# A two-layer expert network with a recurrence between them on one core: the prologue reordered, four staging buffers for weights, integers in the routed rows

## The reference, cut to what matters

```
x = x + 0.5 * ffn(layernorm(x))
x = x + lru(layernorm(x))
x = x + 0.5 * ffn(layernorm(x))

# ffn: top 2 of 8 experts per token
logits = x @ router_w.T + router_b
topk_val, topk_idx = top_k(logits, 2)
weights = softmax(topk_val)
h1, h2 = split(x @ w1[e].T + b1[e])          # 128 -> 2 * 512
out_e  = (silu(h1) * h2) @ w2[e].T + b2[e]   # 512 -> 128
...
# lru: state_t = Lambda * state_(t-1) + B x_t;  y = Re(C state) + D x
```

## Time and profile before

| what | value |
|---|---|
| median of 3 runs | 672.25 us (671.88 to 679.42) |
| profiled execution | 666.18 us, its span 664.4 us |
| prologue, to TensorE's first expert matmul | 99.86 us |
| first expert stage, to the last output scatter | 99.9 to 297 us |
| recurrence and second routing | 297 to 445.2 us |
| second expert stage | 445.2 to 641 us |
| tail | 641 to 664.4 us |
| busy: TensorE, VectorE, ScalarE, GpSimd | 70%, 64%, 53%, 50% of the span |

### The profile page before, as it was taken

The page is one execution under the profiler, slowest core; times in us unless marked ns, Lnnn a source line. Parts: engine busy times, 40 slices in busy tenths (PEclk is TensorE's granted clock), DMA queues, the critical chain, the costliest instruction groups (busy, mean ns, idle before and its releaser), DMA issues.

```text
span 664.4 us, 16357 instructions
## 1 busy us (share of the span) xinstructions
PE 462.8 (70%) x4580; PEld 408.6 (61%) x4580; DVE 423.0 (64%) x1336; ACT 350.9 (53%) x798; POOL 333.4 (50%) x463
## 2 busy tenths in 40 slices
PE   2433007888899999971988783327879799999910
PEld 2433005676699988860878673216769599989910
DVE  6563564656689996737799384145546477776715
ACT  4656233555577777752253431325457477877720
POOL 1277683545656655560002657604557556565640
PEclk9999999879899999985889786558889799999975
DMA  6142362333323222206000101102333223232228
GB/s 195 53 144 72 113 155 63 73 78 80 65 56 67 60 56 52 60 15 227 27 0 18 49 24 56 50 16 61 80 75 84 61 63 69 53 56 61 54 67 313
DMA packets 94552, 50.17 MB, mean 76 GB/s; under 512 B 81902, under 2 KB 84720, under 8 KB 94484
## 3 DMA queue, kind: packets, MB, share of 16 engines
q1 hardware_dynamic: 85396, 32.31, 20.3%
q0 software_dynamic: 9088, 16.94, 8.0%
HBM read 17.25 MB, written 23.24 MB: 61 GB/s over the span
## 4 chain that ended last, share of the span: by engine, by line
PE 55%; DVE 18%; issue 13%; DMA 5%; ACT 3%; another core or an unknown queue 3%; SPq 1%; POOL 1%; POOLq 0%; DVEq 0%; ACTq 0%
PE bank L1188 11%; PE bank L1189 11%; PE bank L1190 11%; PE bank L1210 5%; PE bank L1208 5%; PE bank L1209 5%; DMA yin<-y 3%; DVE bn L658 2%; DVE xres L909 2%; ACT xn L462 2%; PE bank L1070 1%; PE bank L1202 1%; PE bank L1168 1%; DVE w1l L786 1%
## 5 line engine op out<-in xcount | busy, mean ns | idle before, releaser
L424 POOL DMA_INDIRECT y<-yout,dest x156 | 155.3, 995 | 142.3 <-ACT yout L549 105.7
L993 DVE SCALAR_TENSOR_TENSOR act<-bank,bias,gate 128x256 f32<-128x256 f32 x312 | 146.3, 479 | 105.0 <-ACT gate L531 86.6
L403 POOL DMA_INDIRECT rows<-rows,slot_i x128 | 136.2, 1064 | 149.9 <-DVE slot_i L745 110.2
L1188 PE MATMUL bank<-xt_t,w1h 128*128 128x256 f16 x624 | 176.1, 282 | 26.9 <-DVE w2l L786 13.0
L531 ACT ACTIVATE gate<-bank,bias 128x256 f32<-128x256 f32 x312 | 142.3, 479 | 89.1 <-remote 56.0
L1190 PE MATMUL bank<-xt_t,w1l 128*128 128x256 f16 x624 | 175.7, 282 | 4.9 <-issue 4.9
L1189 PE MATMUL bank<-xt_t,w1h 128*128 128x256 f16 x624 | 175.8, 282 | 4.6 <-issue 4.3
L1210 PE MATMUL bank<-w2h,actl 128*128 x624 | 123.5, 223 | 5.8 <-issue 5.8
L1208 PE MATMUL bank<-w2h,wst 128*128 x624 | 124.9, 223 | 3.5 <-issue 3.0
L1209 PE MATMUL bank<-w2l,wst 128*128 x624 | 123.5, 223 | 2.7 <-issue 2.7
L999 DVE TENSOR_TENSOR actl<-act,wst 128x512 f16<-128x512 f32 x156 | 107.8, 691 | 15.2 <-ACT wst L539 10.3
(11 more groups left out here) (200 smaller groups left out, 552.9 us busy)
## 6 DMA issues: line engine op xcount, KB each, us to landing
yin<-y SPq DMA_DIRECT2D x16, 512.0 KB, 4.8
wst<-in_w_t SPq DMA_DIRECT2D x8, 512.0 KB
y<-yout,dest POOLq DMA_INDIRECT x156
rows<-padrow SPq DMA_DIRECT2D x18, 130.0 KB
xres<-in_x SPq DMA_DIRECT2D x8, 256.0 KB, 3.4
wst<-in_w_t SPq DMA_DIRECT2D x8, 256.0 KB
rows<-rows,slot_i POOLq DMA_INDIRECT x128
out<-xres SPq DMA_DIRECT2D x4, 512.0 KB, 6.8
```

The source lines that it names most:

```text
L403: pool.indirect_dma_start(out=rows_dram[f], out_offset=bass.IndirectOffsetOnAxis(ap=slot_i[:, k, f, g, t:t + 1], axis=0), in_=rows[:, k, g ...
L424: pool.indirect_dma_start(out=y_dram[f], out_offset=bass.IndirectOffsetOnAxis(ap=dest[:, t % STEP, r:r + 1], axis=0), in_=yout[:, t % STEP ...
L993: V.scalar_tensor_tensor(act[:, j, :], up_ps[j][:, SLOT:], bias[:, t % STEP, HB + j:HB + j + 1], gate[:, j, :], ALU.add, ALU.mult).then_in ...
L1188: T.matmul(o, w1h[:, bass.ds(at, P)], xt_t[:, t % STEP, 0, :], start=True, stop=False)
```

## The change

- **Staging**: four buffers (`STAGED = 4`) in place of two. `wst` becomes an arena that also holds `acth`, `actl`, `gate` and `act` of the tiles, which had buffers of their own. SP sends the router's two small loads behind x of group 0, then the rest of x, experts 0 to 3, the other ten small loads, and experts 4 to 7, each waiting for `weight_low(e - 4)`.
- **ScalarE's prologue**: `high_part` goes ahead of `transposed`; `weight_high` of experts 0 and 1 goes between them for groups 2 and 3; 2, 3 and 4 behind the second bias; 5, 6 and 7 at the end.
- **VectorE's prologue**: all groups are measured ahead (`measured`, with `mv` for four groups), `scales` runs one group further ahead than it did, and `weight_low` 0, 1, 2 stand behind slots 1, choice 2 and the tile table, 3 to 7 at the end.
- **GpSimd**: 42 rows ahead of tile 0 in stage one, then two behind each of the tiles 0 to 10; as before in stage two (54, then one per tile). The output index is stored as an integer in the row, so `take_meta` is gone: `send_y` and `weighted` read `meta` itself, which has 8 buffers.
- **Tiles** are written out whole on every engine.
- **Recurrence**: `add_outputs(0, 3)` and its statistics move from behind `recurrence(1)` to behind `recurrence(0)`.

```diff
-        wst = sb("wst", [P, 2, 2 * HID + HB * P])
+        wst = sb("wst", [P, STAGED, 2 * HID + HB * P])
+        arena = wst[:, :, :].rearrange("p i w -> p (i w)")
...
-        mv = sb("mv", [P, 2, GT, 2])
+        mv = sb("mv", [P, 4, GT, 2])
...
+                    for dst, src in route:
+                        sp.dma_start(dst, src).then_inc(s_route, 16)
+            for e in range(NE):
+                if e == STAGED:
                     for dst, src in small:
                         sp.dma_start(dst, src).then_inc(s_small, 16)
-            for e in range(NE):
-                if e >= 2:
-
-                    sp.wait_ge(s_wl, 2 * (e - 1))
...
+                if e >= STAGED:
+
+                    sp.wait_ge(s_wl, 2 * (e - STAGED + 1))
...
-                    wait(sp, s_dest, n(1 - STEP))
-                    sp.dma_start(meta[:, t % STEP, :, :],
+                    wait(sp, s_ysent[t % STEP], dma(STEP - METAS, 32))
+                    sp.dma_start(meta[:, t % METAS, :, :],
...
-            def take_meta(t, n, dma):
-
-                pool.wait_ge(s_meta[t % STEP], dma(STEP, 16))
-
-                wait(pool, s_ysent[t % STEP], dma(0, 32))
-
-                pool.sem_inc(s_xgo, 1)
-                pool.tensor_copy(dest[:, t % STEP, :], meta[:, t % STEP, :, 0])
-                pool.tensor_copy(weight[:, t % STEP, :], meta[:, t % STEP, :, 1]).then_inc(s_dest, 1)
...
-                        out_offset=bass.IndirectOffsetOnAxis(ap=dest[:, t % STEP, r:r + 1], axis=0),
+                        out_offset=bass.IndirectOffsetOnAxis(ap=meta_i[:, t % METAS, r, 0:1], axis=0),
...
+                each = [(g, i) for g in range(BATCH) for i in range(TOPK * GT)]
+                ahead = 2 * TOPK * GT + AHEAD_2 if f == 0 else 3 * TOPK * GT + AHEAD
+                for g, i in each[:ahead]:
+                    send_row(f, g, i)
+                later = iter(each[ahead:])
+
+                def tile(t, n, dma):
+
+                    send_y(f, t, n)
+                    for g, i in islice(later, 2 if f == 0 else 1):
                         send_row(f, g, i)
...
             rows_of(0, 0)
             for g in range(BATCH):
                 if g + 1 < BATCH:
-                    rows_of(0, g + 1)
+                    normalise(number["ffn", 0, g + 1])
+                    high_part(0, g + 1)
+                    if g > 0:
+                        weight_high(g - 1)
+                    transposed(number["ffn", 0, g + 1])
+                else:
+                    second_bias()
+                    for e in range(BATCH - 2, NE - 3):
+                        weight_high(e)
                 exp_dif(0, g)
                 second_row(0, g)
...
-                act_e.wait_ge(s_dest, n(1))
+                act_e.wait_ge(s_meta[t % STEP], dma(STEP, 16))
...
+            together(measured(0))
+            together(scales(0, 1))
+            together(measured(1))
+            together(scales(1, 1), measured(2))
+            dve.wait_ge(s_route, 16 * 2)
+            row_parts(0, 0)
+            together(measured(3))
+            together(choose(0, 0), scales(2, 1))
+            weights_and_slots(0, 0)
+            row_parts(0, 1)
+            together(choose(0, 1), scales(3, 1))
+            weights_and_slots(0, 1)
+            weight_low(0)
+            row_parts(0, 2)
+            together(choose(0, 2))
+            weight_low(1)
+            weights_and_slots(0, 2)
+            row_parts(0, 3)
+            together(choose(0, 3))
+            tile_table(0)
+            weight_low(2)
+            tile_list(0)
...
+            for e in range(3, NE):
+                weight_low(e)
...
                     recurrence(0)
+                    add_outputs(0, 3)
+                    measure(number["lru", 0, 3])
```

177 lines of the change are left out of this document (68 added, 109 removed).

## The result

Against the forecast of 655 us (642 to 667) the changed kernel took 686.84 us (683.79 to 688.96, four executions), the kernel before 674.11 (671.88 to 679.42, four): ratio 1.021, 95% interval 1.016 to 1.026. The forecast was wrong. Measured twice more at the end of the study, in twelve executions each, the same kernel took 662.25 us (654.19 to 675.10; ratio 0.987, 0.983 to 0.991) and 664.09 us (655.97 to 672.14; ratio 0.990, 0.985 to 0.995). Both later medians lie in the forecast's range, but not by its sum, as the last part shows. All sets are part of the result.

The account below looks back on a forecast made before the run. It took a chain with waits to bound the prologue and TensorE the first expert stage from 180 us. Terms -16.4 - 1 - 1 + 1.3 = -17.1 us took the median of 672.25 to 655 us, range 642 to 667.

Parts of the forecast that it names:

- ScalarE's five weight waits: Prologue: ScalarE stood 27.6 us in five waits for staged weights; the change was to bring them near zero.
- near 70: Prologue, a rival: the two stalls miss VectorE's chain, first tile near 70 us, -28 us, total 645; chance 0.17.
- the 1.3 us more that was chosen: Recurrence: moving group 3's add_outputs and statistics delays group 0 by 1.3 us; bounds -3.5 and +1.3.
- rival 3: Written-out tiles: code-fetch stalls in the added code cost 30 us with six, so 685 us; chance 0.06.
- What I choose is that both stay: Prologue, VectorE: the 5.5 us at choice 2 and 8.3 us before slots 2 remain in the changed kernel.
- The term of 13.8 us: Prologue: the two stalls kept from the kernel before, 5.5 and 8.3 us, added to VectorE's chain of 67.6 us.
- 83.5: End of the prologue: forecast time in us of the first expert matmul, against 99.86 before, 16.4 us less.
- So stage one keeps its length: First expert stage: GpSimd's share of 5.1 to 5.7 us a tile is below 5.86, so the length stays.
- The bound of +12: First expert stage: upper bound of its change in length, +12 us; the lower bound was -5.
- the choice of -1: First expert stage: the value taken for its change in length, -1 us, between bounds of -5 and +12.
- Rival 2: First expert stage: denser rows delay load 17 or hold outputs at 6.9 us a tile, 11 us back, 666; chance 0.17.
- C: Prologue: VectorE is held at a memory port shared with GpSimd; at 1.8 us a send, load 1 leaves 12 us later.

Follow-up runs that it names:

- the breaks: The changed kernel, with GpSimd waiting in the prologue after every eighth row block until the eight have landed: 659.69 us, 0.986 of the kernel before.
- the gap: The changed kernel, with a 128x400 fill on GpSimd, some 0.5 us without waiting, after every eighth row block in the prologue: 664.99 us in one execution.

## Why the prediction was wrong

**Right.** The routing chain without its waits: slots 2 were asked for at 46 (44.5 forecast), VectorE's first half ran to plan, three of ScalarE's five weight waits went, and where the signals came in time (the breaks and the gap) the first expert matmul was at 66.7 and 68.4, the "near 70" forecast without stalls. The recurrence kept its length within the bounds (148.7 for 148.6, and 143.6 and 144.3 later); the 1.3 us more that was chosen did not show. Code fetch (rival 3) had the right time, 685, by a wrong mechanism: written-out loops alone gave 0.991, and no instruction packet moved in the stall.

**The step that failed first** is "What I choose is that both stay". I took the 5.5 and 8.3 us of the earlier trace rows for fixed costs at a place in VectorE's program. The 8.3 is TensorE's signal coming late under GpSimd's sends. The 5.5 is no single wait and not TensorE's: it is seven gaps of 0.35 to 1.74 us between VectorE's own dependent instructions, such as

```profile
58.08 0.17 DVE L681 SCALAR_TENSOR_TENSOR shift<-mv,rstd 128x8 f32<-128x8 f32 x1 [1.18 <-DVE oh L701]
```

Both kinds move with the sends and have no fixed length. The wait for logits 3 was 28.5 us in the first set's profile; 23.6, 17.3, 16.5, 6.1, 3.3 and 1.9 in other runs with the same routing and the same first 24 sends. The gaps were absent from the first set's trace, where choice 3 and the tile table came after the last send. In the first of the later traces the table came under the last sends and just behind them (the last ended at 79.7, the last gap at 83.8), with 8.9 us of gaps:

```profile
78.17 0.19 DVE L744 SCALAR_TENSOR_TENSOR shift_of<-behind,place 128x33 f32<-128x33 f32 x1 [1.21 <-DVE behind L743]
79.57 0.20 DVE L746 TENSOR_TENSOR step_of<-shift_of 128x33 f32<-128x33 f32 x1 [1.20 <-DVE shift_of L744]
```

In the kernel before, slots 2 came so late that GpSimd ran out of blocks, the one gap in the series of the earlier trace rows:

```profile
74.40 1.68 POOL L403 DMA_INDIRECT rows<-rows,slot_i  x1 [2.53 <-issue]
```

The change makes slots 2 early and takes that pause away; that this made the long wait likelier is an inference from the one gap, not shown. The term of 13.8 us was 36.9 (8.35 and 28.51): 23 us of the 23.6 by which the first matmul missed 83.5. In the first later trace it was 31.0 (4.85, 17.25 and the 8.9), and the first matmul came at 98.5, also past the 92 that the prediction named as its sign of being wrong. Where the wait for logits 3 was 6.1 the first matmul came at 83.1 to 85.8, near the forecast, by luck: the waits there are others than the two that were added.

**The second** is "So stage one keeps its length". The test was GpSimd's capacity, 5.7 us a tile under 5.86. Capacity was not the limit on the whole: the 46 sends of the twelve tiles, at 1.28 each, are some 59 us of 86.5 (an estimate from the sends' spacing). The sends lengthen a tile by holding back TensorE's signals, 1.6 to 2.0 us a block. Twelve tiles took 86.5 us, not 69.5. The first y send came 14.5 us after the first matmul and not the 19.7 of the forecast, which gave 5 us back, and stage one took 9.8 us more. TensorE's granted clock in it was 0.93 on average against 0.96 (behind a wait that ended at 137.7 us its matmuls are recorded at 0.42 us, the lower of its two levels, in place of 0.27), but its busy time is 180.5 us against 178.3, so by that the clock is some 2 us of it. The kernel before with this send order alone lost 10.7 us by the medians (678.36 for 667.63). The bound of +12 held it; the choice of -1 didn't. Rival 2 had the size nearly (11 us) but on GpSimd's queue, at 1.72 us a send; they were 1.27 to 1.30 apart with a few longer ones.

**Stage two** was 5.1 us longer in the first trace. Its sends are the same without the copies of `take_meta`; in the two later traces it was 195.5 and 194.5. So nothing of the change is shown to cost time there.

**The sum as it stands.** By the later traces the first matmul is at 98.5 and 99.2 with waits for logits 3 of 17 us, stage one is 10 us longer, the recurrence 4 to 5 us shorter (as it is in the kernel before with other send orders, 143.7 and 144.6 us, so that is not the change's), and most executions are faster than these two. That the wait is short in those is argued from the times (655 to 660 us beside the 669 and 672 of the two profiles) and was not seen in a trace of this program; a part of the spread is in the kernel before as well, and the run with breaks, whose profile has no such wait, spread over 15 us. What stays open: why all four executions of the first set were slow, what decides how late a signal is (it shows already at logits 2), and why the longest wait outlasted the last send by 5 us. The same program had 28.5 and 17.3 us at this place. Also open is which part of the chip the sends and the late signals share, and whether it is the writing of the sends or the bytes that they move; no run here separates it (near the end of the series, 78 to 80 us, the packets took 20% of the DMA engines' time). C is not excluded as the cause of single long sends: in eleven of the profiles one send of 7.9 to 8.2 us stood in the prologue, each beside VectorE's weight splits. None of the three profiles of the changed kernel has one; there the splits came after the sends.

## What to carry to other kernels

Read the waits that end on "remote" or "issue", behind a TensorE result or inside VectorE's own chain, beside GpSimd's row of the same time: if indirect sends run there, the wait may belong to them and change when they move, so it is no constant of a sum. Keep a series of sends off stretches in which a short chain goes back and forth over TensorE, or give a chain that must cross it pauses: waiting for the landing after each eighth send took the long waits away in the profiles of the three runs that did it, though it brought no time here. Whether 0.5 us without waiting is enough is not shown. Count a send inside a TensorE-bound tile at more than its own time, and put as many as the data allow ahead of the tiles: here all 64 ahead with the new prologue took 0.97 to 0.98 of the kernel before, the best version found.

## What the runs showed of the hardware that was not expected

TensorE's completion reached the waiting engine up to 36.0 us after the recorded end (49.3 to 85.28), the first 31 of them under sends that followed each other without a pause. Under sends its matmuls that start 0.11 us apart otherwise started 0.72 us apart, and VectorE's dependent steps 0.7 in place of 0.20, up to 1.4 us. What was late came 1.0, 2.0, 2.3 and, in the longest case, 5.0 us after the last send. A single execution with a profile does not give the size of such a wait: 28.5, 17.3 and 16.5 us in three executions of one program, whose times go from 654 to 689 us. How much of that range is this wait is not shown.
